# Elastic attention on one core: V's product moved to the end of its step, and its second half paired with that of Q and K

## The reference, cut to what matters

```
qkv = (xp @ w_qkv).reshape(B2, N, 3, H, hd).transpose(2, 0, 3, 1, 4)   # H = 12 heads of hd = 16
q, k, v = (qkv[0] * hmask, qkv[1] * hmask, qkv[2] * hmask)
a = jax.nn.softmax(jnp.einsum('bhnd,bhmd->bhnm', q, k) * scale, axis=-1)
o = jnp.einsum('bhnm,bhmd->bhnd', a, v).transpose(0, 2, 1, 3).reshape(B2, N, C)
o = o @ w_proj + b_proj
```

## Time and profile before

| | |
|---|---|
| median of 3 runs | 1135.11 us (1134.85 to 1139.35) |
| the profiled execution | 1135.37 us, span from first to last instruction 1133.7 us |
| mean granted TensorE clock | 0.996 of full speed |
| busy over the span | PE 96%, PEld 80%, DVE 63%, ACT 67%, POOL 50% |
| elastic attention | from 170.15 us (first scores) to 368.77 us (last output projection) |

### The profile page before, as it was taken

The page is one execution under the profiler, slowest core; times in us unless marked ns, Lnnn a source line. Parts: engine busy times, 40 slices in busy tenths (PEclk is TensorE's granted clock), DMA queues, the critical chain, the costliest instruction groups (busy, mean ns, idle before and its releaser), DMA issues.

```text
span 1133.7 us, 33972 instructions
## 1 busy us (share of the span) xinstructions
PE 1092.4 (96%) x13103; PEld 906.6 (80%) x13103; DVE 717.3 (63%) x2224; ACT 758.4 (67%) x3352; POOL 569.9 (50%) x859
## 2 busy tenths in 40 slices
PE   6999998999998999999999999999999999999998
PEld 4788886777776465479999998999889999998677
DVE  8566566676675125467778777787777777776201
ACT  2256547777776445468788887888788878887331
POOL 2156667445544866436655555455554655456200
PEclk9899999999999999999999999999999999999999
DMA  8100603000000000010000000000000000000001
GB/s 267 25 9 1 133 5 82 2 2 2 2 2 1 1 1 1 1 50 3 3 3 3 2 3 3 2 3 3 2 3 2 3 2 3 3 2 3 11 21 32
DMA packets 34736, 19.86 MB, mean 18 GB/s; under 512 B 24592, under 2 KB 32016, under 8 KB 34576
## 3 DMA queue, kind: packets, MB, share of 16 engines
q1 hardware_dynamic: 34432, 17.20, 5.7%
q10 hardware_dynamic: 144, 0.49, 0.1%
HBM read 15.12 MB, written 1.77 MB: 15 GB/s over the span
## 4 chain that ended last, share of the span: by engine, by line
PE 89%; DVE 6%; ACT 3%; issue 1%; POOL 0%; DVEq 0%; POOLq 0%
PE banks L784 9%; PE banks L1798 8%; PE banks L1758 7%; PE banks L1814 5%; PE banks L1529 5%; PE banks L1786 4%; PE banks L1833 4%; PE banks L2174 3%; PE banks L2128 3%; PE banks L1791 3%; PE banks L1255 2%; PE banks L505 2%; PE banks L1838 2%; PE banks L1276 2%; PE banks L1774 2%; PE banks L1821 2%
## 5 line engine op out<-in xcount | busy, mean ns | idle before, releaser
L2095 POOL TENSOR_TENSOR e_W<-e_W,e_RS 128x384 f32<-128x384 f32 x256 | 205.0, 827 | 258.4 <-DVE e_RS L1976 258.4
L1928 ACT ACTIVATE e_W<-banks,e_MX 128x128 f32<-128x128 f32 x768 | 269.6, 389 | 15.8 <-DVE e_MX L1964 14.6
L1928 ACT ACTIVATION_READ_ACCUMULATOR e_W<-banks,e_MX 128x1 f32 x768 | 175.3, 228 | 0.0
L1922 ACT COPY e_PT<-banks 128x512 f32<-128x512 f32 x128 | 70.2, 588 | 73.4 <-PE banks L1798 73.2
L1798 PE MATMUL banks<-ident,e_W 128*128 128x128 f32 x768 | 107.6, 274 | 2.9 <-POOL e_W L2095 1.4
L784 PE MATMUL banks<-XT,e_wqk 128*128 128x141 f32 x768 | 106.2, 288 | 0.2 <-DVE e_V L1989 0.2
L1503 POOL TENSOR_TENSOR f_W<-f_W,e_RS 128x423 f32<-128x423 f32 x64 | 56.3, 892 | 86.8 <-DVE e_RST L1482 76.5
L784 PEld LDWEIGHTS banks<-XT,e_wqk 128*128 128x128 f32 x768 | 96.0, 190 | 3.0 <-issue 1.2
L1758 PE MATMUL banks<-e_wv,XT 128*128 128x192 f32 (+1 forms) x512 | 95.1, 329 | 0.0
L1798 PEld LDWEIGHTS banks<-ident,e_W 128*128 128x128 f32 x768 | 86.8, 143 | 6.7 <-DVE e_ON L2001 2.9
L1964 DVE TENSOR_REDUCE e_MX<-banks 128x3 f32<-128x384 f32 x128 | 65.4, 553 | 39.8 <-PE banks L1786 39.8
(11 more groups left out here) (325 smaller groups left out, 2713.7 us busy)
## 6 DMA issues: line engine op xcount, KB each, us to landing
xp<-in_patches_dram SPq DMA_DIRECT2D x4, 768.0 KB, 9.2
H<-in_h_dram SPq DMA_DIRECT2D x1, 1728.0 KB, 13.2
out_dram<-H SPq DMA_DIRECT2D x6, 288.0 KB, 2.3
m_hid<-in_e_gu_dram SPq DMA_DIRECT2D x1, 1536.0 KB, 8.7
m_hid<-in_e_o_dram SPq DMA_DIRECT2D x4, 192.0 KB, 7.1
e_wqk<-in_e_qk_dram SPq DMA_DIRECT2D x8, 96.0 KB, 2.6
e_wqk<-in_e_qk_dram SPq DMA_DIRECT2D x24, 32.0 KB, 2.5
e_wv<-in_e_v_dram SPq DMA_DIRECT2D x4, 192.0 KB, 2.6
```

The costliest lines, as they stand in the source:

```text
L1922: nc.scalar.copy(PT[:, 4 * u:4 * u + 4, :], bank[4 + u][:, 0:4 * P]).then_inc(s_pa, 1)
L1928: ex = nc.scalar.activation(W[n % 2][:, t, :], bank[i][:, x * P:(x + 1) * P], ACT.Exp, bias=MX[:, t:t + 1], accum_out=SM[n % 2][:, t:t + 1])
L2095: nc.gpsimd.tensor_tensor(x, x, RS[n % 2][:, 3 * i:3 * i + 3].unsqueeze(2).broadcast_to([P, 3, P]), ALU.mult).then_inc(s_nm, 1)
```

## The change

V of sample n is taken out of the middle of step n and put at its end, into bank 7, where tail scores and output projection live. There it is interleaved with Q and K of sample n+2. The products over channels 0 to 127 come first, three of Q/K and two of V. Of the products over channels 128 to 191, Q/K use rows 0 to 63 of the array and V uses rows 64 to 127, in turns. For that ScalarE writes these channels of `XT` twice, to partitions 0 to 63 and 64 to 127, and V's weights for them are loaded to partitions 64 to 127. VectorE copies V of sample n-1 in step n, behind the copies of Q and ahead of the maxima. New waits: V waits for the tail exponentials of its step and for `finish` of sample n-2, both users of bank 7, and the tail scores wait for the copy of V. The transposes back into bank 6 wait for Q and K of sample n+1 in place of V.

```diff
--- before.py
+++ after.py
@@ -135,7 +135,7 @@
 
         w_a0, w_early, w_ffn, w_fold, w_exp, w_last = (sem(f"weights_{x}") for x in
                                                        ("first", "attention", "ffn", "fold", "experts", "last"))
-        EARLY_W = 16 * (len(QK_PIECES) + 1 + 16)
+        EARLY_W = 16 * (len(QK_PIECES) + 2 + 16)
         early = ctx.enter_context(ExitStack())
 
         def esb(name, shape):
@@ -474,8 +474,10 @@
                 at = 2 * k * P
                 nc.scalar.activation(XT[:, 0, i * P:(i + 1) * P], src[:, at:at + P], ACT.Identity,
                                      scale=vecs[:, v:v + 1], bias=vecs[:, v + 2:v + 3])
-                nc.scalar.activation(XT[0:C1, 1, i * P:(i + 1) * P], src[0:C1, at + P:at + 2 * P], ACT.Identity,
-                                     scale=vecs[0:C1, v + 1:v + 2], bias=vecs[0:C1, v + 3:v + 4]).then_inc(s_nev, 1)
+                for lo in (0, C1):
+                    ev = nc.scalar.activation(XT[lo:lo + C1, 1, i * P:(i + 1) * P], src[0:C1, at + P:at + 2 * P],
+                                              ACT.Identity, scale=vecs[0:C1, v + 1:v + 2], bias=vecs[0:C1, v + 3:v + 4])
+                ev.then_inc(s_nev, 1)
 
         def elastic_q(dve, n, src):
             dve.wait_ge(sf_qkp, n + 1)
@@ -814,7 +816,8 @@
                     sp.dma_start(H[:, :, :], d["h0"].rearrange("(t p) n -> p t n", p=P)).then_inc(st_h, 16)
                     for to, at, n in QK_PIECES:
                         sp.dma_start(f_wqk[:, :, to:to + n], d["f_qk"][:, :, at:at + n]).then_inc(w_early, 16)
-                    sp.dma_start(f_wv[:, :, :], d["f_v"]).then_inc(w_early, 16)
+                    sp.dma_start(f_wv[:, 0, :], d["f_v"][:, 0, :]).then_inc(w_early, 16)
+                    sp.dma_start(f_wv[C1:P, 1, :], d["f_v"][0:C1, 1, :]).then_inc(w_early, 16)
                     heads = d["f_proj"].rearrange("(r x) b n -> r x b n", x=HP)
                     for c, lo, b in ((0, 0, 0), (0, C1, 1), (1, 0, 2), (1, C1, 2)):
                         for r in range(4):
@@ -1215,21 +1218,39 @@
 
                 @block.tensor
                 def _(pe):
-                    def project_qk(n):
-                        if n > 1:
-                            pe.wait_ge(sf_v, 2 * n - 2)
-                        elastic_qk(pe, n, bank[6])
-
-                    def project_v(n):
-                        last = min(n + 2, B)
-                        pe.wait_ge(sf_k, 3 * last)
-                        pe.wait_ge(sf_q, 5 * last)
-                        for i, (k0, nk) in enumerate(QA_SEGS):
-                            for c in range(2):
-                                mm = nc.tensor.matmul(bank[6][0:nk, i * C:(i + 1) * C],
-                                                      XT[:, c, n * SLOT + k0:n * SLOT + k0 + nk], f_wv[:, c, :],
-                                                      start=(i == 0 and c == 0), stop=(c == 1), skip_group_check=True)
-                        mm.then_inc(sf_vp, 1)
+                    def qk_part(n, m, c, rows_c, start, stop):
+                        return nc.tensor.matmul(bank[6][:, m * SEQ:(m + 1) * SEQ], f_wqk[0:rows_c, c, m * P:(m + 1) * P],
+                                                XT[0:rows_c, c, n * SLOT:n * SLOT + SEQ], start=start, stop=stop,
+                                                tile_position=(0, 0), skip_group_check=True)
+
+                    def v_part(n, i, c, lo, start, stop):
+                        k0, nk = QA_SEGS[i]
+                        at = n * SLOT + k0
+                        return nc.tensor.matmul(bank[7][0:nk, i * C:(i + 1) * C], XT[lo:P, c, at:at + nk],
+                                                f_wv[lo:P, c, :], start=start, stop=stop, tile_position=(lo, 0),
+                                                skip_group_check=True)
+
+                    def project_qk_and_v(n):
+                        pe.wait_ge(sf_k, 3 * min(n + 2, B))
+                        pe.wait_ge(sf_q, 5 * min(n + 2, B))
+                        if n + 2 < B:
+                            pe.wait_ge(s_nev, ((n + 2) * SLOT + SEQ - 1) // P + 1)
+                            for m in range(3):
+                                qk_part(n + 2, m, 0, P, m == 0, False)
+                        pe.wait_ge(sf_ex, 5 * n + 2)
+                        if n >= 2:
+                            pe.wait_ge(sf_fin, 2 * (n - 1))
+                        for i in range(2):
+                            v_part(n, i, 0, 0, i == 0, False)
+                        for m in range(3):
+                            if n + 2 < B:
+                                mm = qk_part(n + 2, m, 1, C1, False, True)
+                                if m == 2:
+                                    mm.then_inc(sf_qkp, 1)
+                            if m < 2:
+                                mm = v_part(n, m, 1, C1, False, True)
+                                if m == 1:
+                                    mm.then_inc(sf_vp, 1)
 
                     def scores(n):
                         pe.wait_ge(sf_k, 3 * n + 3)
@@ -1242,8 +1263,8 @@
                                                       KM[n % 2][HP * i:HP * (i + 1), x // 2, :], start=(x == 0), stop=True,
                                                       tile_position=(HP * i, 0), skip_group_check=True)
                         mm.then_inc(sf_sc, 1)
-                        if n >= 3:
-                            pe.wait_ge(sf_fin, 2 * (n - 2))
+                        if n:
+                            pe.wait_ge(sf_v, 2 * n)
                         for i in range(2):
                             mm = nc.tensor.matmul(bank[7][0:NTR, i * SEQ:(i + 1) * SEQ], BQ[n % 2][:, i, :, :],
                                                   KM[n % 2][:, i, :], start=(i == 0), stop=True, skip_group_check=True)
@@ -1296,7 +1317,7 @@
                     pe.wait_ge(s_hm, 6)
                     pe.wait_ge(sf_set, 4)
                     pe.wait_ge(w_early, EARLY_W)
-                    project_qk(1)
+                    elastic_qk(pe, 1, bank[6])
                     for n in range(B + 2):
                         if n == 0:
                             pe.wait_ge(s_nra, TILES - 2)
@@ -1324,8 +1345,6 @@
                             for u in (2, 3):
                                 pe.wait_ge(sf_pa, 3 * n - 4 + u)
                                 transpose(n - 1, u)
-                        if n < B:
-                            project_v(n)
                         if 1 <= n <= B:
                             pe.wait_ge(sf_nm, 5 * n)
                             for u in (4, 5):
@@ -1342,7 +1361,8 @@
                             for k, i in enumerate(LATE2[n]):
                                 forward_second(pe, bank[4][:, 2 * k * P:2 * (k + 1) * P], i)
                         if n in back3_at:
-                            pe.wait_ge(sf_v, 2 * min(n, B - 1) + 2)
+                            pe.wait_ge(sf_k, 3 * min(n + 2, B))
+                            pe.wait_ge(sf_q, 5 * min(n + 2, B))
                             if n - 1 in back3_at:
                                 pe.wait_ge(s_nra, T3 + back3_at[n - 1][-1] + 1)
                             for k, i in enumerate(back3_at[n]):
@@ -1354,10 +1374,10 @@
                                 forward_third(pe, bank[4][:, 2 * k * P:2 * (k + 1) * P], i)
                         if 1 <= n <= B:
                             attend(n - 1)
-                        if n + 2 < B:
+                        if n < B:
                             if n in back3_at:
                                 pe.wait_ge(s_nra, T3 + back3_at[n][-1] + 1)
-                            project_qk(n + 2)
+                            project_qk_and_v(n)
 
                 @block.scalar
                 def _(act):
@@ -1450,7 +1470,7 @@
                             nc.vector.tensor_copy(
                                 VP[n % 2][0:nk, i, :, :].rearrange("p (g a) x -> p g (a x)", a=2)
                                 .rearrange("p g (b d) -> p g b d", d=HD)[:, :, 0:4:3, :],
-                                bank[6][0:nk, i * C:(i + 1) * C].rearrange("p (g b d) -> p g b d", b=2, d=HD)
+                                bank[7][0:nk, i * C:(i + 1) * C].rearrange("p (g b d) -> p g b d", b=2, d=HD)
                             ).then_inc(sf_v, 1)
 
                     def evacuate_attended(n):
@@ -1471,13 +1491,14 @@
                             elastic_q(dve, n + 1, bank[6])
                         if n == 0:
                             add_second(dve, bank[4], REST2)
+                        if 1 <= n <= B:
+                            evacuate_v(n - 1)
                         if n < B:
                             maxima(n)
                         if 1 <= n <= B:
                             evacuate_weights(n - 1, 2)
                             evacuate_weights(n - 1, 3)
                         if n < B:
-                            evacuate_v(n)
```

## The result

The changed kernel takes 1165.01 us (median of 4, 1162.89 to 1168.99) against 1134.98 of before: ratio 1.0266, interval 1.0241 to 1.0292. It is slower, as forecast, but by 30 us and not by 19.6, and 1165 lies above the range of 1147 to 1162. The profiled execution took 1166.39 us.

The account below looks back on a forecast made before the run. The chain through VectorE's copies, not TensorE's passes (96% busy), was taken to bound the attention steps; 16.9 + 0.2 + 2.5 = 19.6 us on 1135.37 gave 1155.0, with the median 0.26 lower 1154.7, range 1147 to 1162.

Parts of the forecast that it names:

- V is free where it stands, and the move puts it on the chain: Elastic attention: V fills time in which TensorE waits for VectorE anyhow; moved, each step grows by T4's delay, 1.30 us.
- The new end of a step, 2.47: TensorE's Q/K with V at a step's end: 2.47 us where Q/K alone took 1.54, so +0.93.
- 0.80 and 0.20: At a step's end on TensorE: 0.80 us for the paired matmuls in halves, 0.20 for going into the halves.
- The 0.89: Paired Q/K and V matmuls taken pass beside pass under program order: 0.89 us, making the sum 1.2 us larger.
- VectorE, and T4 at 8.15: V's copies on VectorE hold the tail scores until 4.74; T4 starts 8.15 us after Q/K, 1.30 later than now.
- T4's wait grows to about 2 us: TensorE's wait in each step for VectorE's copy ahead of T4 grows from 0.5 to about 2 us.
- the sum of 19.6: Total added time: 16.9 us over steps 2 to 14, 0.2 in step 1, 2.5 at the ends of steps 14 and 15.
- The hidden edits: Three edits priced at nothing: ScalarE's second write (up to 7 us if uncovered), the load in two parts, V's wait for `finish`.
- No overlap: Rival on the end of a step: the unequal Q/K and V pairs don't run side by side; 1162 us, chance 0.13.
- Bank 7: Rival: `finish` or the tail exponentials hold V up at bank 7; 1159 us with 0.3 us late, chance 0.05.
- The way back found elsewhere: Rival: VectorE's copy of T2 comes earlier than thought and the step absorbs V; 1135 us, chance 0.06.
- TensorE as the bound: Rival: in the steps only TensorE's passes count and the wait ahead of T4 goes; 1126 us, chance 0.05.

Follow-up runs that it names:

- e4_no_v: The kernel before with V's product and its copies left out of the elastic attention; 1145.49 to 1168.83 us, ratio 1.0158.
- e3_move_only: The change without the halves: V at the end of its step in bank 7, behind unsplit Q/K, channels 128 to 191 written once; 1157.47 us, ratio 1.0213.
- e1_fill: The change with four more matmuls, read by nobody, between T3 and T4 where V stood before; 1151.84 us, ratio to before 1.0159.
- e7_write_twice: The kernel before with only channels 128 to 191 written twice in the first attention, as the change has it; 1133.76 us, ratio 0.9993.
- e6_before_early: The kernel before with VectorE's maximum of banks 2 and 3 moved behind its copies of T2 and T3; 1127.37 us, ratio 0.9935.
- e2_same_half: The change with V's second products on rows 0 to 63 as well, so that no pair can overlap; 1171.57 us, ratio 1.0329.
- e5_after_early: The change with VectorE's maximum of banks 2 and 3 moved behind its copies of T2 and T3; 1145.60 us, ratio 1.0092.

## Why the prediction was wrong in size

- **V is free where it stands, and the move puts it on the chain.** Right: e4_no_v shows the first, e3_move_only the second, at 1.30 us a step.
- **The new end of a step, 2.47.** Measured 2.49. The pairs run in their halves each at its own pace, 0.12 a pass for Q/K (273.97 to 274.09) and 0.16 for V (273.97 to 274.13); what I took as 0.80 and 0.20 is 274.66 - 273.74 = 0.92 with part of the mode changes in it. The 0.89 that I drew from the rule on program order (the Trainium skill, TensorE: Matmul & The Clock Gate, "Step-by-step: what each phase is for") didn't follow from it: the matmuls do start in program order here (Q/K at 273.74, V at 273.75), but neither half waits for the other's end. The overlap is worth 0.64, not 0.57.
- **VectorE, and T4 at 8.15.** Measured 8.04: VectorE's copies started at 2.59 and not 2.67 and took 2.00 and not 2.07, and the tail scores started at 4.64 (276.81 - 272.17), held by V's copy. Each step costs 1.19, not 1.30, which makes the sum of 19.6 too large by 13 times 0.11, 1.4 us; e1_fill has 17.7 in all.
- **T4's wait grows to about 2 us.** Right, 1.8 us, and this is where the prediction failed. I took the wait as idle time without a further price, and read the clock of the kernel before ("at full clock") as if it would stay. The step that failed is this term, put at nothing without a reason: the fall of TensorE's clock to half behind such waits. e1_fill takes it out by giving the engine something to do, and 13.2 us go (1165.0 to 1151.8), more than the 10.3 by which the forecast fell short. The rest is offset by the cheaper step, 17.7 against 19.6, and by a median of before that was 0.8 us lower in that comparison.
- **The hidden edits**: the second write (e7_write_twice) and V's wait for `finish`, which is no wait of TensorE's from 190 to 360 us. In step 0 V does wait for the tail exponentials, 1.75 us, hidden as forecast: T0 of step 1 still waits 0.24 us for GpSimd, and from the first scores to the second it is 8.85 us against 8.76. What was not forecast is that the clock falls behind this wait too.
- **The rivals.** No overlap: out by the rows above. Bank 7: out, since from 190 to 360 us no wait stands ahead of V. The way back found elsewhere: out, T4 comes 1.19 later. TensorE as the bound: out by e4_no_v, and its own condition, T2's copy in time, is what e6_before_early made; then the time did fall.

The half clock shows also in single steps. The step of 18.00 us is 4.60 longer than the 13.40 of e1_fill in the same place. Between the first and the last scores the change has 203.5 us and e1_fill 194.5; from the last scores to the feed-forward layer it is 27.68 against 22.34. That is 9.0 + 5.3 = 14.3 us; the 2.0 more behind it I can't place, since there both have a clock of 1.00. Up to the first scores the change is 2.9 us shorter than the profiled execution before. That one has a stretch of half clock at 36 to 42 us, and none of the other profiled executions has it, so it belongs to that run and not to the kernel.

What stays open is which steps the clock falls in. From step 2 on every step of e2_same_half, e3_move_only, e4_no_v and the change has the same wait of 1.8 us, and the clock falls in some, in other ones in each kernel, and for different lengths. The 13 falls in their steps all start 1.2 to 1.9 us after the end of T4's wait, but most such waits have none. Falls with no such wait ahead are few: at 36 us before, at 385 us in e3_move_only, and the last two of e5_after_early. I ran nothing that tells what decides between two like steps, nor why the change, with halves, lost more clock than e3_move_only.

## What to carry to other kernels

Work that fills a wait is free, and taken away from there it isn't saved: ask of each piece of work whether the chain that ended last goes through it, and only then how many passes it has. When a change makes an engine's wait longer, price the clock as well as the wait, since here that was 13 us beside 18. And look at the other side of the wait first: VectorE did a maximum of 1.0 us ahead of the copy that TensorE stood waiting for, and swapping them made the kernel before 7 us faster, where moving TensorE's work made it 30 us slower.

## What the hardware showed that I had not expected

- TensorE with 21 us less to do made the kernel slower: 1145 to 1169 us against a median of 1134 (e4_no_v), at mean clocks of 0.964 to 0.986.
- Waits of 0.5 us in each step of the attention left TensorE's clock at 1.00 (before, e1_fill), as did waits of 0.86 and 0.47 from 181 to 375 us (e5_after_early). Waits of 1.8 us in steps of 12 to 14 us brought it to 1.2 GHz in some of them: 0.92 on the mean from 167 to 398 us in the change.
- Two halves of the array with matmuls of unequal length, 141 and 192 columns, go on independently: 0.12 and 0.16 us a pass at the same time, no slower than each over the whole array.
